# The copies of the transposed input out of PSUM, moved from ScalarE to VectorE in an attention and channel-mix layer

## What is computed

```python
q = x @ Wq + bq;  k = x @ Wk + bk;  v = x @ Wv + bv      # 16 heads of 64
q = q * cos + rotate_half_interleaved(q) * sin           # k likewise
ctx = softmax(q @ k.T / sqrt(64)) @ v
x = layernorm(x + ctx)
xr, xk = mu_r * x + (1 - mu_r) * x_prev, mu_k * x + (1 - mu_k) * x_prev
x = layernorm(x + sigmoid(xr @ W_r.T) * (square(relu(xk @ W_k.T)) @ W_v.T))
```

## Time and profile before

| | us |
|---|---|
| median of the runs | 4368.11 (4296.78 to 4439.44, 2 runs) |
| the profiled execution | 4297.33 |
| its span, slowest core (core 3) | 4295.1 |
| spans of the eight cores | 4281.4 to 4295.1 |
| TensorE busy | 3090.7 (72%) |
| ScalarE busy | 2476.0 (58%) |
| VectorE busy | 1011.7 (24%) |
| GpSimd busy | 291.3 (7%) |

### The profile page before, as it was taken

How to read it: one execution, slowest core, us unless ns; L and a number is a source line. 1 busy time by engine, 2 the same in 40 slices (tenths; PEclk the granted TensorE clock), 3 DMA queues, 4 the chain that set the end, 5 groups by cost and what they waited for, 6 DMA issues and landing times.

```text
span 4295.1 us, 53310 instructions; the slowest of 8 cores (4281.4 to 4295.1 us)
## 1 busy us (share of the span) xinstructions
PE 3090.7 (72%) x19520; PEld 1146.2 (27%) x19520; DVE 1011.7 (24%) x2391; ACT 2476.0 (58%) x2367; POOL 291.3 (7%) x292
## 2 busy tenths in 40 slices
PE   1554778878887888788788878887888788205555
PEld 1222222222222222222322222222222222102222
DVE  2222622212221221222122212221221000035453
ACT  0443067757775777576667757775777688101111
POOL 0111100010010001000100010010001000121110
PEclk9666899989998999899899989998999899658877
DMA  7443411111101110211021111101110000230110
GB/s 219 171 157 128 142 64 60 40 51 50 50 30 60 50 54 17 71 58 49 17 74 50 40 50 50 50 30 60 50 59 12 11 1 1 70 127 33 47 58 39
DMA packets 80348, 262.76 MB, mean 61 GB/s; under 512 B 6242, under 2 KB 40290, under 8 KB 61410
## 3 DMA queue, kind: packets, MB, share of 16 engines
q1 hardware_dynamic: 77282, 242.59, 16.7%
q0 software_dynamic: 2816, 16.78, 1.0%
HBM read 225.27 MB, written 34.08 MB: 60 GB/s over the span
## 4 chain that ended last, share of the span: by engine, by line
PE 44%; ACT 27%; issue 6%; DVE 6%; DMA 4%; POOL 1%; DVEq 1%; ACTq 0%; SPq 0%; POOLq 0%
ACT pt_sb L771 25%; PE ps_c L756 14%; PE ps_stB L745 6%; PE ps_b L559 5%; PE ps_b L597 5%; PE ps_stA L745 4%; PE ps_d L1260 2%; PE ps_d L1234 1%; PE ps_c L864 1%; PE ps_b L661 1%; DMA xf_b<-xT_spill 1%; DVE ctxT_f L789 1%; PE ps_b L919 1%; PE ps_c L796 1%; DMA ctxg<-ctx_spill 1%
## 5 line engine op out<-in xcount | busy, mean ns | idle before, releaser
L771 ACT ACTIVATE pt_sb<-ps_stA,mhat_sb 128x1024 bf16<-128x1024 f32 x1024 | 1141.2, 1115 | 419.9 <-PE ps_c L756 256.8
L771 ACT ACTIVATE pt_sb<-ps_stB,mhat_sb 128x1024 bf16<-128x1024 f32 x1024 | 1141.8, 1115 | 270.3 <-PE ps_c L756 245.3
L756 PE MATMUL ps_c<-pt_sb,v_aug 128*65 128x512 bf16 x3968 | 1240.1, 394 | 0.0
L745 PE MATMUL ps_stB<-qT,kT 64*64 64x512 bf16 x4096 | 428.1, 404 | 187.7 <-ACT pt_sb L771 181.0
L745 PE MATMUL ps_stA<-qT,kT 64*64 64x512 bf16 x4096 | 430.6, 406 | 142.1 <-ACT pt_sb L771 126.6
L756 PEld LDWEIGHTS ps_c<-pt_sb,v_aug 128*65 128x65 bf16 x3968 | 279.5, 110 | 456.4 <-issue 456.4
L745 PEld LDWEIGHTS ps_stB<-qT,kT 64*64 64x64 bf16 x4096 | 136.2, 104 | 607.9 <-issue 602.1
L745 PEld LDWEIGHTS ps_stA<-qT,kT 64*64 64x64 bf16 x4096 | 135.9, 104 | 579.0 <-issue 572.0
L652 POOL TENSOR_TENSOR ksq<-kT 128x512 bf16<-128x512 bf16 x112 | 115.4, 1037 | 2384.0 <-DVE kT L588 2370.0
L559 PE MATMUL ps_b<-xf_b,wkv_sb 128*128 128x512 bf16 x896 | 232.4, 406 | 50.7 <-DMA xf_b<-xT_spill 50.7
L573 DVE TENSOR_SCALAR kpre<-ps_b,bk_sb 128x512 bf16<-128x512 f32 x112 | 84.1, 751 | 636.2 <-PE ps_b L559 636.2
(11 more groups left out here) (142 smaller groups left out, 2187.0 us busy)
## 6 DMA issues: line engine op xcount, KB each, us to landing
xf_b<-xT_spill SPq DMA_DIRECT2D x128, 1024.0 KB, 4.8
xst_f<-x_full SPq DMA_DIRECT2D x16, 2048.0 KB, 8.0
xT_spill<-xfT_st POOLq DMA_DIRECT2D x16, 1024.0 KB, 4.5
ctx_spill<-ctx_hp SPq DMA_DIRECT2D x8, 1088.0 KB, 5.9
xo_c<-x_own SPq DMA_DIRECT2D x17, 512.0 KB, 4.3
ctxg<-ctx_spill SPq DMA_DIRECT2D x17, 512.0 KB, 3.5
xst_f<-x_own SPq DMA_DIRECT2D x4, 2048.0 KB, 10.4
out<-xo_c SPq DMA_DIRECT2D x16, 512.0 KB, 2.6
```

The source lines that it names most:

```text
L745: r = e.matmul(ps_st[g].rearrange("p (b n) -> p b n", b=2) [half * 64:half * 64 + 64, h, 0:qn], kT2[buf][h * 64:h * 64 + 64, c * 128 + hal ...
L756: r = e.matmul(ps_c[h][0:65, 0:qn], v_aug[buf].rearrange("p (k x) -> p k x", k=KC) [:, cp, h * 65:h * 65 + 65], pt_sb[:, (cp % 4) * 1024 + ...
L771: sB.op("scalar", lambda e, g=g, c=c, hp=hp: e.activation(pt_sb[:, (c % 4) * 1024:(c % 4) * 1024 + 1024], ps_st[g][:, 0:1024], AF.Exp, bia ...
```

## The change

The copy out of `psa_tr` into `xfT_st` is issued on VectorE in place of ScalarE. Its operands, its line and what it depends on stay as they were.

```diff
-                sA.op("scalar", lambda e, pb=pb, s=s, kt=kt: e.copy(
+                sA.op("vector", lambda e, pb=pb, s=s, kt=kt: e.tensor_copy(
                     xfT_st[kt % 2][:, :].rearrange("p (c t) -> p c t", c=NCC)
                     [:, :, s * 128:(s + 1) * 128],
                     psa_tr[pb][:, :].rearrange("p (c n) -> p c n", c=NCC)),
                     reads=[trk(f"psa_tr{pb}")], writes=[trk(f"xfT_st{kt % 2}")])
```

## The result

The changed kernel takes 1.0062 times as long as the kernel before, with a 95% interval of 1.0040 to 1.0084. On 4297 us that is 27 us more, 17 to 36. The profiled execution took 4317.42 us against 4297.33, 20 us more; a second profiled execution of each took 4329.55 and 4292.16. Over all runs the medians are 4325.74 (25 runs) and 4297.83 (24 runs).

The account below looks back on a forecast made before the run. The prediction took TensorE's own queue, its work plus round trips waiting for GpSimd's square, as the first part's bound. 4297.33 + 17 (copies' places) - 0 (ScalarE's relief) + 2 (clock) = 4316 us; range 4296 to 4390.

Parts of the forecast that it names:

- What bounds the part: First part, 105 to 418 us: TensorE's own queue, its work plus 40 waits for GpSimd's square, 130.7 us.
- What goes: ScalarE loses 64 copies, 64.8 us, valued at nothing; a cast and load 13 us earlier, also valued at zero.
- The copies' places: VectorE copies standing ahead of backs 0, 2, 3 and 4 delay L430: 2.15 us a period, 17.2 us in all.
- first term: The delay of L430 by copies ahead of backs: taken as 17 us, with bounds of 0 and 37.
- The clock: TensorE's front after back 0's longer wait runs less at the upper clock level: +2 us taken.
- the two signs: Clock term on the front after back 0: at most 6.6 us slower, or 5 us the other way.
- The sum: Whole kernel: 4297.33 + 17 - 0 + 2 = 4316 us.
- the likeliest case: The forecast of 4316 us itself, whole kernel, chance 0.70, own range 4304 to 4328.
- My 4387: Whole kernel: median 71 us above the sum if the changed kernel's runs scatter as the two shown.
- 1 (out of the way): Copies end before each rotation does, waits stay at 3.59 us; time 4297, chance 0.10.
- 2 (ScalarE's copies on the path, 4277): ScalarE's copies were on the path, so VectorE's quicker ones take 20.6 us off; chance 0.05.
- 3 (the clock stays down): TensorE's clock no longer rises in each period's opening fronts and transposes: 39 to 46 us, time 4356, chance 0.12.

Follow-up runs that it names:

- experiment 3: All 64 copies on VectorE as in the changed kernel, but those ahead of a back issued behind it in VectorE's queue; 1.0013 times the kernel before.
- experiment 4: The changed kernel with each of its VectorE copies done twice; 1.0138 times the kernel before.
- experiment 6: TensorE's sum of squares two backs later, closing maximum also later; against the kernel before 0.9817 with copies on ScalarE, 0.9809 with them on VectorE.
- experiment 8: Six unread matmuls behind each rotation on TensorE; first cast to second part's first load 281.5 us on the kernel before, 310.9 on the changed kernel.

## Why the prediction was right or wrong

- *What bounds the part*: right. Experiments 3 and 4 move the waits as the queue says, and experiment 6 takes 85 us off by moving one instruction.
- *What goes*: right. ScalarE's 64 us bought nothing, and the earlier cast neither helped nor hurt (experiment 3).
- *The copies' places*: right place by place, and a little too small. The forecast was 2.15 us a period, and over the eight periods of core 5 it is 2.49. Back 0 cost 0.97 (I said 0.88), back 1 0.04 (0), back 2 0.48 (0.32), back 3 0.36 (0.32), back 4 0.63 (0.63). In all 19.9 us for 17.2. The step that failed is the size of this first term: the walk over one period of the old trace was taken as if it stood for all. In back 2 the rotation runs at the upper level in three of the eight periods, in 0.38 us and not 0.63, and then more of the copy is uncovered (row 214.66 above); and a few single waits carry 0.35 us on top.
- *The clock*: +2 forecast, +2.5 to +3 measured in the stretch (183.1 and 183.8 against 180.7 and 180.8). Of the two signs that I allowed it was the plus. That the size came so near is in part luck. Over periods 2 to 8 of core 5 the front behind back 0, the only one in my term, takes 3.2 us more and the sums of squares 1.3 more, but the rotations take 1.8 less and the second fronts 1.2 less; the prediction had none of these three.
- *The sum*: 19 us forecast, 22.4 measured in the stretch, 20 between the two profiled executions, and 27 (17 to 36) over all runs. The time of 4316 is thus some 5 to 10 us under the measured level, a slowdown of 0.44% where 0.62% was measured. Of the 8 us between 19 and 27, about 3 are the first term (19.9 for 17) and 0.5 the clock's. The other 4 to 5 would lie behind the first load, where I forecast no change; the two pairs of profiled executions show 0 and 10 us there, the interval of the 27 takes in the 22.4, and the cause, if it is more than scatter, stays open. Mechanism and sign were right, and the size of the sum was short. Calling this "within 2%" was right, but it is not no change: the interval excludes 1.
- *The base*: the sum was set on the profiled execution's 4297.33, while the time on record was 4368.11. Against that time 4316 reads as 1.2% faster, which the text did not mean and which did not come. The profiled execution was the better base. My 4387, the time with the scatter of the two runs, falls short by the same 8 us: 4368.11 with the measured ratio is 4395, which is above the range's end of 4390.
- *Rivals*: 1 (out of the way) and 2 (ScalarE's copies on the path, 4277) are refuted by the interval and the waits. The rule of the Trainium skill cited there (page Perfetto Trace Analysis, section Optimizing Scalar/DVE Operations) held for the duration, 692 against 1013 ns, and not for the time. 3 (the clock stays down) did not come: in periods 2 to 8 of the changed kernel on core 5 the second and third fronts run at 1.89 us, and on core 3 in all but periods 2 and 3. The front behind back 0 did go down: it takes some 3.2 to 3.6 us in every period of core 5, and before it took between 1.9 and 3.6.
- *The range*: the likeliest case's own 4304 to 4328 held the median of all runs, 4325.74, and one of the two profiled executions; the other took 4329.55. The upper end of 4390 was there for rival 3 and for the scatter of two runs.

## What to carry to other kernels

Before moving an instruction to a less busy engine, look at what stands behind it in that engine's queue and who waits for that; the busy shares say nothing of it. Here VectorE was 24% busy, but 48 of its 64 new copies stood right ahead of the instruction for which TensorE sits still, and of their 33 us 20 were added to TensorE's waits. If such an instruction must move, put it behind the awaited one (experiment 3, no loss), or better, move the waiting engine's wait (experiment 6, 85 us off the stretch); and look again after that, because the free places change with the bound.

## What the runs showed of the hardware

- A VectorE copy out of PSUM beside GpSimd's square slows neither: 1.48 us for two copies and 1.03 for the square (experiment 3). Two such copies take 1.48 us in the earlier trace rows as well, and the mean of the 32 large squares is 1034 ns in experiment 3 and 1033 in the kernel before.
- Unread matmuls in TensorE's waits shortened the stretch by 30 us: the mean granted clock in it rose from 0.66 to 0.87, and more than half of the gain is in the transposes and in the first front of a period (experiment 8).
- Some single waits are longer by 0.35 us with nothing in the trace to account for it: 2.30 us and not 1.95 before, 4.84 and not 4.49 in back 0 after. The extra lies between VectorE's sum and the start of GpSimd's square. It falls on the same waits on cores 3 and 5 and, on core 5, again in the second execution of either kernel, so it is not chance. I did not find its cause.
